# Flamingo block on one core: x normalised outright by pairs of blocks, weights and transfers of the attention rearranged

## The reference

```python
# 8 blocks (B) of 128 rows (S), width 128 (D); E = 16 experts, 2 per row
def attn(k, v, q):                        # k = v = ctx_1024
    kp, vp, qp = k @ Wk.T, v @ Wv.T + bv, q @ Wq.T + bq
    probs = softmax(qp @ kp.T / sqrt(D))
    return (probs @ vp) @ Wo.T + bo
x = x + tanh(g_xattn) * attn(ctx, ctx, layernorm(x))
x = x + tanh(g_ffn) * ffn(layernorm(x))   # one shared swiglu expert, hidden 512,
                                          # plus the best 2 of 16 experts, hidden 128
```

## Time and profile before

| | us |
|---|---|
| median of 3 runs | 69.86 (69.68 to 70.09) |
| the profiled execution | 69.69 |
| its span | 66.8 |
| TensorE busy | 58.6 (88%) |
| VectorE busy | 40.2 (60%) |
| ScalarE busy | 22.3 (33%) |
| GpSimd busy | 11.3 (17%) |

### The profile page before, as it was taken

The page is one execution under the profiler, slowest core; times in us unless marked ns, Lnnn a source line. Parts: engine busy times, 40 slices in busy tenths (PEclk is TensorE's granted clock), DMA queues, the critical chain, the costliest instruction groups (busy, mean ns, idle before and its releaser), DMA issues.

```text
span 66.8 us, 1072 instructions
## 1 busy us (share of the span) xinstructions
PE 58.6 (88%) x319; PEld 40.6 (61%) x319; DVE 40.2 (60%) x163; ACT 22.3 (33%) x49; POOL 11.3 (17%) x32
## 2 busy tenths in 40 slices
PE   2988798999598999999999999999989999999300
PEld 0326566989083549494977475575879947658200
DVE  0029058749861136999959568971467567597910
ACT  0603676773549950313413303113030330320000
POOL 5702600862883000080000000000000000000000
PEclk9999999999999999999999999999999999999999
DMA  0799950000000000000000000388980000003232
GB/s 0 173 305 205 369 231 22 0 0 0 0 0 0 10 0 0 5 0 0 0 0 0 0 0 0 118 241 226 295 286 21 5 0 0 0 5 103 64 102 70
DMA packets 5352, 4.77 MB, mean 71 GB/s; under 512 B 352, under 2 KB 5216, under 8 KB 5344
## 3 DMA queue, kind: packets, MB, share of 16 engines
q1 hardware_dynamic: 4528, 4.20, 19.9%
q10 hardware_dynamic: 816, 0.47, 3.6%
HBM read 4.15 MB, written 0.52 MB: 70 GB/s over the span
## 4 chain that ended last, share of the span: by engine, by line
PE 72%; DMA 8%; DVE 5%; ACT 4%; issue 2%; SPq 1%; DVEq 1%; ACTq 0%
PE bank L841 11%; PE bank L832 11%; PE bank L835 10%; PE bank L904 10%; DMA params<-in_attn_params_dram 8%; PE bank L916 7%; PE bank L733 4%; PE bank L787 3%; DVE acc L696 3%; PE bank L774 3%; PE bank L899 3%; PE bank L847 2%; PE bank L810 2%; PE bank L806 1%; PE bank L757 1%
## 5 line engine op out<-in xcount | busy, mean ns | idle before, releaser
L442 ACT ACTIVATE silu_t<-bank 128x512 f32<-128x512 f32 x14 | 8.4, 597 | 24.8 <-PE bank L832 11.8
L571 DVE TENSOR_TENSOR hid<-silu_t,bank 128x512 f32<-128x512 f32 x14 | 9.6, 685 | 5.7 <-ACT silu_t L442 2.8
L841 PEld LDWEIGHTS bank<-shared_sb,hid 128*128 128x128 f32 x64 | 8.2, 192 | 2.4 <-issue 2.2
L832 PE MATMUL bank<-x2nT,shared_sb 128*128 128x512 f32 x16 | 8.3, 603 | 0.3 <-ACT x2nT L434 0.3
L841 PE MATMUL bank<-shared_sb,hid 128*128 128x128 f32 x64 | 8.5, 276 | 0.0
L835 PE MATMUL bank<-x2nT,shared_sb 128*128 128x512 f32 x16 | 8.2, 596 | 0.0
L904 PE MATMUL bank<-x2nT,dense_w 128*128 128x512 f32 x16 | 7.5, 593 | 0.0
L475 DVE BATCH_NORM_STATS2 stats<-x_sb 128x6 f32<-128x128 f32 x8 | 1.9, 278 | 6.5 <-DMA x_sb<-in_x_dram 6.5
L729 PE MATMUL bank<-fill 128*128 128x512 bf16 x11 | 4.4, 537 | 1.3 <-POOL fill L319 1.3
L835 PEld LDWEIGHTS bank<-x2nT,shared_sb 128*128 128x128 f32 x16 | 3.0, 190 | 3.4 <-issue 3.3
L696 DVE SCALAR_TENSOR_TENSOR acc<-bank,dense_gates,acc 128x128 f32<-128x128 f32 x16 | 4.5, 344 | 0.8 <-PE bank L916 0.7
(11 more groups left out here) (137 smaller groups left out, 85.8 us busy)
## 6 DMA issues: line engine op xcount, KB each, us to landing
place_w<-in_routed_w_dram SPq DMA_DIRECT2D x8, 192.0 KB, 3.8
shared_sb<-in_shared_w_dram SPq DMA_DIRECT2D x1, 768.0 KB, 8.0
x_sb<-in_x_dram SPq DMA_DIRECT2D x2, 256.0 KB, 5.1
dense_w<-in_routed_w_dram SPq DMA_DIRECT2D x2, 192.0 KB, 3.4
ctx_sb<-in_ctx_dram ACTq DMA_DIRECT2D x1, 256.0 KB, 4.4
ctx_sb<-in_ctx_dram SPq DMA_DIRECT2D x1, 256.0 KB, 6.7
out_dram<-acc SPq DMA_DIRECT2D x1, 256.0 KB, 2.4
out_dram<-acc SPq DMA_DIRECT2D x2, 128.0 KB, 2.4
```

The source lines that it names most:

```text
L442: nc.scalar.activation(silu_t[:, i % 2, :], UP[i % 2][0][:, :], ACT.Silu).then_inc(silu_ready, 1)
L571: nc.vector.tensor_tensor(hid[:, i % HID_RING, :], silu_t[:, i % 2, :], UP[i % 2][1][:, :], ALU.mult)\
L832: nc.tensor.matmul(UP[i % 2][0][:, :], w1s[:, j * P:(j + 1) * P], xt, start=True, stop=True).then_inc(gate_done, 1)
L841: last = nc.tensor.matmul(BASE[t][:, b * P:(b + 1) * P], hid[:, i % HID_RING, b * P:(b + 1) * P], w3s[:, j, :], start=(j == 0 and b == 0), ...
```

## The change

All eight blocks of x are normalised outright (mean subtracted, times 1/deviation) before they are transposed: the first four by VectorE, in pairs, with GpSimd's power in between, the last four by GpSimd. So Wq is not centred, `score_bias` and the scaling of scores are gone, and the bias of bq, now one column, is added by ScalarE when it copies gT. `vo_w` is copied without tanh; tanh(g_xattn) is multiplied in where the values leave TensorE (VectorE for the first half, ScalarE for the second). `vo_bias` is added to the second half's values on GpSimd, after ScalarE's copy, and no longer to the residual; `vo_ready`, for which `share_up(0)` waits, is now counted there. bo has a transfer of its own, issued by GpSimd. On SP's queue x's second half is second and Wv, bq, bv third; Wo comes with Wq and Wk. There are eight early fill matmuls for seven, two more and one more a little later, and three fewer around the x2n transposes. Scores, values, probabilities and attention of the first two pairs stand in another order.

```diff
@@ SP, GpSimd @@
             sp.dma_start(x_sb[:, halves(0), :], x_dram[:, halves(0), :]).then_inc(x_loaded[0], 16)
+            sp.dma_start(x_sb[:, halves(1), :], x_dram[:, halves(1), :]).then_inc(x_loaded[1], 16)
             sp.dma_start(params[:, 3 * D:], attn_params[:, 3 * D:]).then_inc(params_loaded[1], 16)
-            sp.dma_start(params[:, 0:D], attn_params[:, 0:D]).then_inc(params_loaded[2], 16)
-            sp.dma_start(x_sb[:, halves(1), :], x_dram[:, halves(1), :]).then_inc(x_loaded[1], 16)
...
             pool.memset(fill[:, :], 1.0).then_inc(fill_ready, 1)
+            pool.dma_start(bo_row[:, :], row_params[0:1, 0:D]).then_inc(bo_loaded, 16)
...
-                pool.tensor_tensor(x_biased[:, :, :], x_sb[:, halves(1), :],
-                                   vo_bias[:, None, :].to_broadcast([P, HALF, D]), ALU.add).then_inc(x_biased_ready, 1)
+                pool.wait_ge(vo_last_copied, 1)
+                pool.tensor_tensor(vo[:, halves(1), 0:D], vo[:, halves(1), 0:D],
+                                   vo_bias[:, None, :].to_broadcast([P, HALF, D]), ALU.add).then_inc(vo_ready, 1)
...
@@ ScalarE @@
-            act.dma_start(params[:, D:3 * D], attn_params[:, D:3 * D]).then_inc(params_loaded[0], 16)
+            act.dma_start(params[:, 0:3 * D], attn_params[:, 0:3 * D]).then_inc(params_loaded[0], 16)
...
             exponentials(0)
-            act.wait_ge(vo_bias_done, 1)
-            nc.scalar.mul(vo_bias[:, :], bank[3][:, 0:128], tanh_g[:, 0:1]).then_inc(vo_bias_ready, 1)
+            act.wait_ge(probs_turned, 1)
+            nc.scalar.copy(probsT[:, twos(0), :], by_block(TURNED_PROBS[0][:, 0:256])).then_inc(probsT_ready, 1)
             exponentials(1)
-            for p in range(2):
-                act.wait_ge(probs_turned, p + 1)
-                nc.scalar.copy(probsT[:, twos(p), :], by_block(TURNED_PROBS[p][:, 0:256])).then_inc(probsT_ready, 1)
             act.wait_ge(ctx_turned, 2)
             nc.scalar.copy(ctxT[:, halves(1), :], by_block(bank[4][:, :])).then_inc(ctxT_ready, 1)
+            act.wait_ge(probs_turned, 2)
+            nc.scalar.copy(probsT[:, twos(1), :], by_block(TURNED_PROBS[1][:, 0:256])).then_inc(probsT_ready, 1)
...
-            exponentials(2)
             act.wait_ge(x2n_turned, 3)
             nc.scalar.copy(x2nT[:, 4, :], bank[4][:, 0:P]).then_inc(x2nT_ready_too, 1)
+            exponentials(2)
             exponentials(3)
@@ VectorE @@
             dve.wait_ge(x_loaded[0], 16)
+            for p in range(2):
+                x_stats(2 * p)
+                x_stats(2 * p + 1)
+                x_moments(2 * p, 2)
+            for b in range(HALF):
+                normalise_x(b)
             dve.wait_ge(x_loaded[1], 16)
             for b in range(HALF, B):
                 x_stats(b)
+            dve.wait_ge(xn_turned, 2)
+            nc.vector.tensor_copy(xT[:, twos(1), :], by_block(bank[1][:, 0:256])).then_inc(xT_second_ready, 1)
+            x_moments(HALF, HALF)
+            row_max(0)
             dve.wait_ge(vo_done, 1)
             dve.wait_ge(vo_bias_ready, 1)
-            nc.vector.tensor_tensor(vo[:, halves(0), 0:D], by_block(bank[2][:, :]), vo_bias[:, None, :].to_broadcast([P, HALF, D]), ALU.add)\
+            nc.vector.scalar_tensor_tensor(vo[:, halves(0), 0:D], by_block(bank[2][:, :]), tanh_g[:, 0:1],
+                                           vo_bias[:, None, :].to_broadcast([P, HALF, D]), ALU.mult, ALU.add)\
                 .then_inc(vo_ready, 1)
+            row_max(1)
@@ TensorE: its list after the change, up to the second half @@
+            keep_warm(8, bank[7])
+            pe.wait_ge(ident_ready, 1)
+            pe.wait_ge(params_loaded[0], 16)
+            nc.tensor.matmul(bank[2][:, 0:128], wq_sb, wk_sb, start=True, stop=True).then_inc(qk_done, 1)
+            nc.tensor.transpose(bank[3][:, 0:128], wo_sb, ident[:, :]).then_inc(wo_turned, 1)
+            keep_warm(2, bank[7])
             pe.wait_ge(ctx_loaded[0], 16)
             turn(bank[4], ctx_sb, 0, HALF).then_inc(ctx_turned, 1)
             pe.wait_ge(params_loaded[1], 16)
             pe.wait_ge(qk_ready, 1)
+            nc.tensor.matmul(bank[2][:, 0:1], wk_sb, bq_col, start=True, stop=True).then_inc(u_done, 1)
+            pe.wait_ge(woT_ready, 1)
+            nc.tensor.matmul(bank[3][:, 0:128], wv_sb, woT[:, :], start=True, stop=True).then_inc(vo_w_done, 1)
+            keep_warm(1, bank[7])
+            pe.wait_ge(xn_ready, 2)
+            turn(bank[0], xn, 0, 2).then_inc(xn_turned, 1)
+            pe.wait_ge(bo_loaded, 16)
+            pe.wait_ge(consts_ready, 2)
+            pe.wait_ge(vo_w_ready, 1)
+            nc.tensor.matmul(bank[3][:, 0:128], bv_col.to_broadcast([P, P]), woT[:, :], start=True, stop=False)
+            nc.tensor.matmul(bank[3][:, 0:128], ones_mat[0:1, :], bo_row[:, :], start=False, stop=True).then_inc(vo_bias_done, 1)
...
+            turn(bank[1], xn, 2, 2).then_inc(xn_turned, 1)
...
+            values(0, bank[2], 0, 2)
+            pe.wait_ge(gT_first_ready, 1)
+            score(0)
...
+            values(0, bank[2], 2, 2).then_inc(vo_done, 1)
+            pe.wait_ge(gT_second_ready, 1)
+            score(1)
...
             turn(bank[4], ctx_sb, HALF, HALF).then_inc(ctx_turned, 1)
+            turn_probs(0)
...
+            attend(0)
+            turn_probs(1)
...
+            attend(1)
```

More of the change, by code:

```diff
@@ L144, in flamingo_block @@
         acc = sb("acc", [P, 1 + B, D])
-        params_loaded = [sem(f"params_loaded{i}") for i in range(3)]
+        params_loaded = [sem(f"params_loaded{i}") for i in range(2)]
         rows_loaded = sem("rows_loaded")
+        bo_loaded = sem("bo_loaded")
         x_loaded = [sem(f"x_loaded{h}") for h in range(2)]
@@ L362, in normalise_odd @@
                 pool.wait_ge(x2_rstd_ready, p + 1)
[L363 removed]
+                pool.tensor_scalar(x2n[:, b, :], x2[:, b, :], neg_mean[:, 1, b:b + 1], rstd[:, 1, b:b + 1],
                                    ALU.add, ALU.mult).then_inc(x2n_ready_too, 1)
+            pool.wait_ge(consts_ready, 2)
             inverse_x_deviation(0)
             inverse_x_deviation(1)
[L368 to L371, removed]
+            pool.wait_ge(x_moments_ready, B)
+            pool.tensor_scalar(neg_mean[:, 0, halves(1)], mean_var[:, 0, halves(1), 0], -1.0, 0.0, ALU.mult, ALU.add).then_inc(x_neg_mean_ready, 1)
+            pool.wait_ge(x_var_ready, 3)
+            pool.tensor_tensor(rstd[:, 0, halves(1)], var_eps[:, 0, halves(1)], neg_half[:, :], ALU.pow).then_inc(x_rstd_ready, 1)
+            pool.wait_ge(x_neg_mean_ready, 1)
+            pool.wait_ge(x_rstd_ready, 3)
+            for b in range(HALF, B):
+                pool.tensor_scalar(xn[:, b, :], x_sb[:, b, :], neg_mean[:, 0, b:b + 1], rstd[:, 0, b:b + 1],
+                                   ALU.add, ALU.mult).then_inc(xn_last_ready, 1)
             normalise_odd(0)
@@ L427, in _ @@
                 .then_inc(gT_last_ready, 1)
             act.wait_ge(vo_done, 2)
-            nc.scalar.copy(vo[:, halves(1), 0:D], by_block(bank[3][:, :])).then_inc(vo_ready, 1)
+            nc.scalar.mul(vo[:, halves(1), 0:D], by_block(bank[3][:, :]), tanh_g[:, 0:1]).then_inc(vo_last_copied, 1)
             act.wait_ge(x2n_turned, 1)
             nc.scalar.copy(x2nT[:, 1:3, :], by_block(bank[6][:, 0:256])).then_inc(x2nT_ready_too, 1)
-            exponentials(2)
             act.wait_ge(x2n_turned, 3)
@@ L744, in _ @@
+            nc.tensor.transpose(bank[3][:, 0:128], wo_sb, ident[:, :]).then_inc(wo_turned, 1)
+            keep_warm(2, bank[7])
             pe.wait_ge(ctx_loaded[0], 16)
             turn(bank[4], ctx_sb, 0, HALF).then_inc(ctx_turned, 1)
-            pe.wait_ge(params_loaded[2], 16)
-            nc.tensor.transpose(bank[3][:, 0:128], wo_sb, ident[:, :]).then_inc(wo_turned, 1)
             pe.wait_ge(params_loaded[1], 16)
             pe.wait_ge(qk_ready, 1)
-            nc.tensor.matmul(bank[2][:, 0:128], wk_sb, bq_col.to_broadcast([P, P]), start=True, stop=True).then_inc(u_done, 1)
+            nc.tensor.matmul(bank[2][:, 0:1], wk_sb, bq_col, start=True, stop=True).then_inc(u_done, 1)
@@ L756, in _, with values @@
-            pe.wait_ge(ctxT_ready, 1)
-            nc.tensor.matmul(bank[7][:, :], u_mat[:, :], ctxT[:, halves(0), :], start=True, stop=True).then_inc(score_bias_done, 1)
-            for p in range(2):
-                pe.wait_ge((gT_first_ready, gT_second_ready)[p], 1)
+            pe.wait_ge(xn_ready, 4)
+            turn(bank[1], xn, 2, 2).then_inc(xn_turned, 1)
+            def values(h, dst, b0, n):
+                for b in range(b0, b0 + n):
+                    last = nc.tensor.matmul(dst[:, b * D:(b + 1) * D], ctxT[:, HALF * h + b, :], vo_w[:, :], start=True, stop=True)
+                return last
@@ L760, in _, with score @@
+            def score(p):
                 for b in (2 * p, 2 * p + 1):
@@ L762, in _ @@
                 last.then_inc(scores_done, 1)
-                if p == 0:
-                    pe.wait_ge(woT_ready, 1)
```

(50 more changed lines are left out.)

142 lines of the change are left out of this document (47 added, 95 removed).

## The result

| | us |
|---|---|
| before, median of 21 executions beside it | 70.09 |
| after, median of 21 executions | 70.02 |
| ratio after to before, undisturbed executions | 1.0082 (1.0051 to 1.0113) |
| the same ratio in a second session (e1 below) | 1.0185 (1.0127 to 1.0243) |
| median span of after in the two sessions | 67.3, 67.95 |

The change makes the kernel slower, by about 0.6 us in one session and 1.3 us in the other. In some executions, whatever the kernel, the time is some per cent longer; the ratios and spans leave these out, and the two medians hide the difference only because more executions of before than of after were among them.

A forecast was written before the change was run, and what follows sets the result against it. TensorE's list up to `share_up(0)` was taken as the bound, begun by a transfer: L 8.3 plus 13.8 gives 22.1 against 20.94, +1.15. Added to 69.86 this forecast 71.0 us, range 69.6 to 71.9.

The forecast's parts named there:

- L: Landing of Wv, bq, bv, which TensorE awaits after the ctx transposes: 8.3 us, kept between 7.39 and 8.9.
- From L to `share_up(0)`: TensorE's work after L, through scores, attend(1) and x2n transposes, up to share_up(0): 13.8 us.
- The score tail: From row_max(1) to attend(1)'s end, reordered: 3.23 us against 2.81 today, so 0.4 lost.
- add_bias: GpSimd's addition ahead of share_up(0): ends 4.9 of 5.35 us after attend(1), hidden with 0.4 to spare.
- Normalising outright: x's normalising before its transposes: all four first blocks ready at about 7.9, beside the wait if L is over 7.1.
- bo's transfer: Separate 0.5 KB load from GpSimd: lands between almost at once and 6.8, needed at 9.2, so costs nothing.
- Rival A: The landing does not bind, L at or under 6.9: share_up(0) at 20.7, -0.25, 69.6 us; chance 0.15.
- Rival C: TensorE idles from 6.9 to 8.3, its clock falls, costing about 1 us more: 72.0; chance 0.07.
- Rival B: No change: L near 7.4, share_up(0) at 21.2, +0.25, 70.1 us; chance 0.12.

The follow-up runs named there:

- e1: The changed kernel, unedited, run again in a second session: ratio to the kernel before 1.0185.
- e2: The changed kernel with Wv, bq, bv second and x's second half third on SP's queue: ratio to the kernel before 1.0095.
- e12: The kernel before with Wo loaded with Wq and Wk on ScalarE's queue and eight early fills for seven: ratio 1.0090.
- e5: The changed kernel with the old order of its tail (exponentials, turned probabilities, ctxT): ratio to the kernel before 1.0013.
- e7: The changed kernel with the edits of e6 and e5 together: ratio to the kernel before 0.9891.
- e6: e2 plus, on VectorE, xT's second copy moved ahead of the statistics of x's second half: ratio to the kernel before 0.9969.
- e3: The kernel before with x's second half moved to second place on SP's queue, nothing else: ratio 1.0387.
- the profiled execution: The changed kernel, unedited, in the first session's profile, where TensorE's clock fell: 74.06 us, span 71.9.
- the best version: The kernel of e10, with three edits to the changed kernel: ratio to the kernel before 0.9825.
- e4: The changed kernel with four more fill matmuls ahead of the wait for Wv, bq, bv: 69.79 us, ratio to the kernel before 1.0094.
- e8: e3 with seven fill matmuls between the ctx transposes and the wait for Wo: ratio to the kernel before 1.0028.
- e9: The kernel of e7 run again in another session: ratio to the kernel before 0.9899.
- e10: e9 with share_up(0) no longer waiting for GpSimd's addition (vo_ready 2): ratio to the kernel before 0.9825.
- e11: The kernel before with Wo loaded with Wq and Wk on ScalarE's queue, seven early fills kept: median 71.34 us for 69.68.

## Why the prediction came out as it did

The direction was right and by its own mechanism: `params_loaded[1]`, moved behind x's second half, is the transfer that TensorE waits for next. 71.0 was forecast (+1.15); the two sessions gave +0.6 and +1.3. An ordinary execution of the first session took 70.0, 1.0 less than forecast. Two things make that up: the base was taken as 69.86, where 70.0/1.0082 gives 69.4, and the change was put 0.6 too high. The median span of 67.3 less the 46 us behind `share_up(0)` puts it at about 21.3 there, an estimate, for there is no trace of such an execution; the points below go by e1, from the second session. Point by point:

- **L.** Taken as 8.3 from a count of bytes (8.63), with 7.39 as the lower bound. The profiles of the unchanged queue order gave 7.72, 7.74, 7.84 and, in the execution with the fallen clock, 8.64. In the first three it is nearer to the lower bound than I took it: 8.3 is 0.5 us too much. The count also failed the other way: it gives x's second half, third in e2 and e12, the same 8.6, and it landed at 9.57 and 9.46. In these runs the bytes ahead on the queues give a landing only to within 1 us.
- **From L to `share_up(0)`.** 13.8 forecast, 14.17 measured. L to the end of attend(1) was 8.95 for 8.43, the rest 5.22 for 5.35. The missing 0.5 lies in the early part, and scores(1) start at L+4.98 for L+4.43: by the chain of waits u and vo_w took 0.38+0.33 for 0.46, the first g 0.63 for 0.43, scores 0.61 for 0.50. Little of it is due to the wait: in e2, without it, u is 0.10 shorter from its start to vo_w's (0.14 for 0.24), but the first g takes as long (0.54 from start to start, 0.53 in e1). Why it takes longer than its row is open. That 22.1 was forecast and 21.89 measured is partly luck: L was 0.6 too high and the sum behind it 0.4 too low.
- **The score tail.** row_max(1) to attend(1)'s end: 3.23 forecast, 13.45 to 16.67 = 3.22 measured. Its share of the loss, put at 0.4, was 0.32 when undone (e5), where add_bias then decided.
- **add_bias.** End of the addition 4.9 after attend(1), forecast; 21.54-16.67 = 4.87 measured. Hidden with 0.35 to spare, and it does decide once the chain is shorter (e5, e7), with `normalise_odd(1)` ahead of it, as the prediction feared.
- **Normalising outright.** Forecast as covered by the wait; e6, without the wait, still has the u product at 6.6 and starts xn's transposes at 7.25, right behind the fill, so there it is covered without it too. What the removal of score_bias and of the scaling is worth by itself was not isolated.
- **bo's transfer.** Landed 5.2 to 5.4 us after its issue (1.25) in the changed kernel, at about 6.5, inside the bounds. The estimate from the Trainium skill (DMA: Bandwidth & Descriptors, Anatomy of one DMA — SWDGE (gpsimd) path), 3.3, was half of it; here the measurement decides, and it changed nothing, since bo is wanted at 8.9. Its issue took 0.73 us of GpSimd and ident was ready by 2.7: covered.
- **Rival A** (the landing does not bind) was made by hand in e6: `share_up(0)` at 20.72 against the 20.7 worked out, a match of two errors: u started at 6.59 for 6.9, and 14.13 followed for 13.8. **Rival C** was given 0.07; it is real, once in 27 executions (one of 69 executions of before had a low clock too), and dearer than priced: of the 3.45 us between 21.89 and 25.34, 0.9 are L and 2.5 the clock, where I had put 1. The step that failed there is the length: I let the lower level last 2.5 us, and it lasted 6.8. The rule of the Trainium skill (TensorE: Matmul & The Clock Gate, Part 1: The HAM clock gate (the "warmup" mystery)), that an idle engine goes back to 1.2 GHz, agrees with the falls after 1.69 and 2.08 us of idle time; after 0.62 and 1.17 us these traces show none. Rival B (+0.25) is the nearest in the first session by its place for `share_up(0)`, 21.2 for some 21.3.

## What to carry to other kernels

A transfer that is moved up moves another down, and what counts is who stands behind each wait in an in-order list: here VectorE's copy queued behind statistics of data that it does not need was as dear as the wait that it replaced. When a wait is taken away, look in the same trace at the next landing and at what is queued behind its consumer, and move that work ahead. A wait in TensorE's list as long as those of e3 and of the profiled execution (1.69 and 2.08 us) should be priced twice, once for itself and once for the clock behind it. And a gain in time should be compared with the gain in span: here more than half of the best version's 1.2 us is not in the part of the execution that the argument explains.

## What the runs showed of the hardware

- After idle stretches of 1.69 and 2.08 us TensorE's granted clock fell to half and stayed there for some 3.4 us (e3) and 6.8 us (after), although the engine had work all the while. After 0.62 us (e1) and 1.17 us (e5) it did not fall.
- bo's 0.5 KB, issued by GpSimd beside the large loads, took 4.4 to 5.4 us to land, longer than the 192 KB issued by ScalarE just before (3.0 to 3.3).
- The time around the span is not constant. Its median was 2.7 to 3.0 us in the kernel before and 2.5 to 2.6 in the changed one, but 3.2 in e3, 3.1 in e12, 2.2 in e6, 1.9 in e4 and 1.8 in e8, and for one and the same kernel 2.0 in e7 and 2.45 in e9. Why is open; in e4 to e10 it makes the ratio lower than the span does.
- The profile's granted clock reads 1.00 from the start, though the duration of passes shows the lower level until about 6 us in the kernel before (1.06 us for four transposes) and until about 10 in e11 (0.85 us for L753's two passes at 9.46, 0.43 for two of the same size, L752, in the earlier trace rows) and in e8's profile (2.99 us for seven fills).
